# A planner's two rules in a kernel of attention and experts: when a side job may take its bank, and from when its result counts

## What is computed

```python
q, k, v = (split_heads(x @ W + b) for W, b in ((Wq, bq), (Wk, bk), (Wv, bv)))
attn = einsum(q, k) / sqrt(32) - slope[h] * (T - 1 - key)      # causal
x = layernorm(x + (softmax(attn) @ v) @ Wo + bo)
p = softmax(x @ Wr + br);  e = argmax(p)
y = (silu(x @ Wg[e]) * (x @ Wu[e])) @ Wd[e] * p[e]
x = layernorm(x + y)
```

## Time and profile before

| | us |
|---|---|
| median of 3 runs | 1257.86 (1256.21 to 1259.7) |
| the profiled execution, its own time | 1257.54 |
| its span, first to last instruction | 1255.8 |
| attention units | about 27 to 485 |
| tail between attention and experts | about 485 to 541 |
| experts | about 541 to 1240 |

### The profile page before, as it was taken

One profiled execution on the slowest core, in us unless ns is written; L12 is line 12 of the kernel. 1 busy time (PEld: TensorE's weight loads), 2 busy tenths in 40 slices (PEclk: granted clock), 3 DMA queues, 4 the chain that ended last, 5 costly groups with the idle time before them and its releaser, 6 DMA issues.

```text
span 1255.8 us, 27816 instructions
## 1 busy us (share of the span) xinstructions
PE 1165.1 (93%) x8697; PEld 1063.2 (85%) x8697; DVE 768.6 (61%) x1978; ACT 570.4 (45%) x1395; POOL 307.3 (24%) x443
## 2 busy tenths in 40 slices
PE   6998998999899987499999999999999999999994
PEld 5888888887888875498998899899989988998993
DVE  3676767676767776456546655664665465456665
ACT  4676766765666673043323332332333232323344
POOL 5400201201020122353213311330331133123336
PEclk9999999999999998589999999999999999999997
DMA  8223223222322240271322223122313222231302
GB/s 274 62 52 79 71 67 103 54 60 68 94 52 64 68 123 35 61 200 44 93 68 62 75 79 91 51 85 68 93 51 91 72 60 76 72 98 51 85 33 103
DMA packets 109685, 100.11 MB, mean 80 GB/s; under 512 B 12847, under 2 KB 81839, under 8 KB 109552
## 3 DMA queue, kind: packets, MB, share of 16 engines
q1 hardware_dynamic: 104784, 87.85, 24.8%
q0 software_dynamic: 3040, 9.18, 2.2%
q10 hardware_dynamic: 1728, 1.31, 0.3%
HBM read 64.74 MB, written 9.18 MB: 59 GB/s over the span
## 4 chain that ended last, share of the span: by engine, by line
PE 76%; DVE 6%; POOL 5%; ACT 4%; issue 4%; DMA 3%; SPq 1%; ACTq 0%; DVEq 0%; POOLq 0%
PE bank L805 35%; PE bank L583 14%; PE bank L830 10%; PE bank L721 4%; PE bank L704 4%; POOL up_lo L1455 4%; PE bank L817 3%; PE bank L693 2%; DMA up_raw<-in_Wu_dram 2%; SPq L475 1%; ACT probs L913 1%; DVE probs L1153 1%; PE bank L730 1%; PE bank L681 1%; ACT up_hi L945 1%
## 5 line engine op out<-in xcount | busy, mean ns | idle before, releaser
L805 PE MATMUL bank<-up_hi,xsT_hi 128*128 x1216 | 356.2, 293 | 5.7 <-POOL up_lo L1455 4.6
L805 PE MATMUL bank<-up_lo,xsT_hi 128*128 x1216 | 344.6, 283 | 0.0
L805 PE MATMUL bank<-up_hi,xsT_lo 128*128 x1216 | 344.5, 283 | 0.0
L1455 POOL TENSOR_TENSOR up_lo<-up_raw,up_hi 128x256 fp32r<-128x256 f32 x241 | 169.9, 741 | 477.8 <-ACT up_hi L945 477.6
L1294 DVE SCALAR_TENSOR_TENSOR h_tok<-bank,row_weight,silu 128x128 f32<-128x128 f32 x304 | 93.4, 347 | 292.3 <-ACT silu L1009 292.3
L805 PEld LDWEIGHTS bank<-up_hi,xsT_hi 128*128 128x128 f32 x1216 | 233.0, 192 | 12.3 <-issue 12.0
L805 PEld LDWEIGHTS bank<-up_hi,xsT_lo 128*128 128x128 f32 x1216 | 233.7, 192 | 0.3
L805 PEld LDWEIGHTS bank<-up_lo,xsT_hi 128*128 128x128 f32 x1216 | 233.1, 192 | 0.0
L1009 ACT ACTIVATE silu<-bank 128x256 f32<-128x256 f32 (+1 forms) x160 | 59.6, 373 | 364.5 <-PE bank L805 364.5
L1311 DVE TENSOR_TENSOR y<-bank,y 128x512 f32<-128x512 f32 x295 | 198.5, 688 | 0.5
L913 ACT ACTIVATE probs<-probs,neg_max 128x512 f32<-128x512 f32 (+3 forms) x256 | 136.5, 558 | 56.4 <-DVE neg_max L1153 55.4
(11 more groups left out here) (168 smaller groups left out, 2083.8 us busy)
## 6 DMA issues: line engine op xcount, KB each, us to landing
up_raw<-in_Wg_dram SPq DMA_DIRECT2D x64, 256.0 KB, 3.5
up_raw<-in_Wu_dram SPq DMA_DIRECT2D x64, 256.0 KB, 4.1
down_raw<-in_Wd_dram SPq DMA_DIRECT2D x64, 256.0 KB, 2.7
k_stack<-qk_hi SPq DMA_DIRECT2D x128, 64.0 KB, 2.0
q_stack<-qk_hi SPq DMA_DIRECT2D x128, 64.0 KB, 2.0
k_stack<-qk_lo SPq DMA_DIRECT2D x64, 64.0 KB, 2.0
q_stack<-qk_lo SPq DMA_DIRECT2D x64, 64.0 KB, 2.0
x_tok<-in_x_dram SPq DMA_DIRECT2D x3, 1024.0 KB, 5.5
```

Of the source, the lines that this page charges most:

```text
L805: mm = pe.matmul(bank[:, n * 2 * P:(n + 1) * 2 * P], a[:, s, k, :], up_w[w][k][:, :, :].rearrange("p a f -> p (a f)")[:, bass.ds(at, 2 * P ...
L1455: pool.tensor_tensor(up_w[1][k][:, e, :], up_raw[:, idx % NUPS, k, :, :].rearrange("p g f -> p (g f)"), up_w[0][k][:, e, :].bitcast(F32), ...
```

## The change

A bank that a job is to take must now have been flushed in an earlier unit for half 0, and in this unit or earlier for half 1 (`plan.flushed.get(prior, U) + (1 - half) > u` refuses it). And results flushed in unit u enter `ready` only after half 1 of unit u, so they can be used from unit u+1 on; in the last units (from 186) they still enter between the halves. Everything else, the jobs, their sizes and the budget, stays. No instruction is added or removed; the side jobs of units 36 to 179 move by half a unit to several units, and a few jobs change places in the row (`OP` 0 goes behind `V` 3,1; `logit` 0 and `logit` 3 go behind `Q` 7 and `V` 4,1). The next sequence has the same moves 48 units later.

```diff
--- before.py
+++ after.py
@@ -168,7 +168,9 @@
             if not left:
                 if any(k not in ready for k in needs(queue[0])):
                     return
-                if any(plan.bank[j] == len(plan.number) % 2 for j in pending):
+
+                prior = plan.used.get(len(plan.number) % 2)
+                if prior is not None and plan.flushed.get(prior, U) + (1 - half) > u:
                     return
                 now_job = queue.popleft()
                 plan.add(now_job, 2)
@@ -231,10 +233,13 @@
             work(u, 0, owed() / (PER_GROUP - step))
         if u > VLAG + PER_HEAD + 2 and (u - VLAG - 3) % PER_HEAD == 0:
             ready.add(("o", (u - VLAG - 3) // PER_HEAD - 1))
+
+        if u >= U - PER_GROUP // 2:
+            ready.update(fresh)
+        if u < U:
+            work(u, 1, owed() / (PER_GROUP - step))
         ready.update(fresh)
         fresh.clear()
-        if u < U:
-            work(u, 1, owed() / (PER_GROUP - step))
     plan.rest = list(left) and [(now_job, left[0][0])] or []
     plan.rest_jobs = list(queue)
     plan.pending = list(pending)
```

## The result

| | before | after |
|---|---|---|
| median | 1258.78 (4 runs, 1256.21 to 1266.14) | 1243.01 (4 runs, 1240.69 to 1246.4) |
| ratio of runs | | 0.9868, 95% interval 0.9844 to 0.9893 |
| profiled execution, span | 1255.8 | 1244.6 |
| waits of PE for DVE's side takes, units 37 to 179 | 20.9 in 23 | 6.6 in 11 |
| start of unit 37 to start of unit 180 | 350.4 | 335.5 |

The forecast was 1245.5, range 1238 to 1255. The change gains 15.8 us by the medians. The last two rows of the table come from the starts of PE's score rows in the timeline; they say that the whole gain, 14.9 us in this profile, lies in the units whose side work moved. The profiled execution of the changed kernel reached unit 37 3.4 us later than that of the kernel before (104.2 against 100.8), in code that the change leaves alone; so its span shows less than the stretch does.

What follows compares the result with a forecast made beforehand. PE, working in order, was taken to set the pace, its idle waits for DVE's takes being winnable. Terms 12.45 + 2.1 (clock) - 2.2 (new waits) = 12.35 off 1257.86 gave 1245.5 us, range 1238 to 1255.

Steps and rivals of the forecast that it cites:

- What bounds the kernel: Units from 100 to 452 us: PE sets the pace; its waits for DVE's side takes are 20.9 us, 24.4 with allowance.
- xT and K, first sequence: Units 37 and 38: the xT pair in half 1 saves 0.45 us, K one half later 0.4, together 0.85.
- OT to OP 3 and the router rows: Units 58 to 87, again 106 to 135: shorter waits from moved jobs, 0.7, 2.35, 0.3 and 1.7 us a sequence.
- DVE's backlog at xT: Units 84 to 87: DVE can no longer catch up in PE's long stops, so waits of 0.5, 1.1 and 0.7 us.
- New waits: Units without side work go from 15 to 23; eight more at 0.27 us waiting for ACT cost 2.2 us.
- Clock: Granted clock falls at 302.4 and 333 us both go with shorter stops: 2.1 us gained, ends 0 and 3.1.
- Last sequence: Units 152, 162, 164 and 176: 1.5 us less of the 3.3 us of waits there.
- x in time: x load issued one iteration later, at 80, stays hidden: some 7 us from issue to need, 1.5 us to spare.
- The signs: Expected if right: waits 8 to 12 us, `OP` 2 under 0.6, `logit` 2 0.7 to 1.1, stretch some 12 us shorter.
- The waits move and do not go: Rival, chance 0.17: DVE's row begins no sooner, so the next job waits what the last saved; 1252.5 us.
- All vanish: Rival, chance 0.05: DVE runs ahead as PE's row is spread out, 24.4 + 2.1 us goes; 1231 us.
- the slower side: Clock rival, chance 0.07: light PE stretches at bare units make the clock fall, up to 1.54 us each; 1264 us.

Runs made afterwards that it cites:

- the first rule alone: Kernel before with only the bank change: a bank may be taken one half later, results still count from the flush's own unit; ratio 0.9887.
- `xT` moved back: Changed kernel with the bank condition lifted for the four xT jobs, so the second pair stands in half 0 again; one run, 1243.59 us.
- moments late: Changed kernel with DVE's moments of an OP placed behind the biased scores, not ahead; ratios 0.9846 and 0.9854, medians 1241.2 and 1240.9 us.
- x in parts: Changed kernel with the third and fourth sequence's x loads cut into four, each issued once its quarter's last reading OP is taken; 1243.3 us.

## Why the prediction was right, and where its steps were off

The direction, the place and the mechanism were right: 1243.0 lies in the range, 2.5 under the forecast. By its own steps:

- **What bounds the kernel.** Right. 14.3 of the 20.9 us of waits went, and the stretch is 12.7 shorter besides the clock.
- **xT and K, first sequence: 0.85.** Measured 0.55. The 0.45 for the `xT` pair was wrong: with the first rule alone it is 0.01, and with `xT` moved back nothing is lost. All of it is the bare unit put into the 3.88 us in front of `K`.
- **OT to OP 3 and the router rows: 5.05 a sequence** (0.7 + 2.35 + 0.3 + 1.7), less 1.1 for new waits, 3.95. Measured 5.0 and 5.6 in units 49 to 97, and in 97 to 145 8.05, of which the kernel before lost 2.2 to the clock: 5.9. The stops before `OP` 1, `OP` 2 and `OP` 3 did not shrink to 0.15, 0.46 and 0.4, they vanished, and `logit` 2 kept 0.33 and not 0.8. (The single stretches of 12 units can't be set against the terms: `OP` 0 and `logit` 3 moved across their borders.)
- **DVE's backlog at xT**: 0.5, 1.1 and 0.7 were put at units 84, 85 and 86 to 87; the rows have 0, 0.47 + 0.82 and 0.76. Right in kind and size.
- **New waits: 2.2.** This term was mis-sized. It took one stop of 0.27 for each new bare unit; ACT's exponentials cost 0.2 in all, and the products with v 0.26 and 0.35 (units 169 and 178) outside the units already counted. Together with the stops at `OP` and `logit`, two points up, it makes up the 2.5 to 3.1 by which the stretch was better than 12.35.
- **Clock: 2.1.** Right: 1.55 and, from units 121 to 133 of the kernel before being 0.63 longer than 73 to 85, 0.6; and both profiles of the changed kernel have no fall there. Not every fall comes back at its place, so a profile of the kernel before may hold more or fewer.
- **Last sequence: 1.5.** Measured 1.25.
- **x in time.** Right in outcome, by 0.2 us; the working took the landing time of the kernel before, 5.5 us, and here it was 6.5.
- **The signs.** Four of its six signs of being right came: `OP` 2's stop under 0.6, the `xT` stops as long as before, the stretch shorter (14.9, put at some 12), the experts unchanged. Two did not, both on the side of too little gain: the waits for side takes sum to 6.6 and not 8 to 12, and `logit` 2 waits 0.33 and not 0.7 to 1.1. By the medians the gain is 15.8, 3.4 more than the 12.35 of the sum. That the number is only 2.5 off is in part luck: with its fourth run the median of the kernel before came out 0.9 higher.
- **The rivals.** "The waits move and do not go" holds for the `xT` chain and was seen nowhere else. "All vanish" did not come, and the slower side neither: 23 bare units, no fall.

## What to carry to other kernels

When an in-order engine stops for a result that another engine is just about to take, place the job by what the taking engine has in front of it, not by when the producer is done: here half a unit of other work, together with a take that no longer stood behind 0.9 us of DVE's own work, ended a whole stop of 1.8 us. Before moving a job, find out whether its stop is a lone wait or a link in a serial chain (start to start stayed at 3.87 to 3.88 us in three kernels): there only work put inside the chain counts. And follow what else is released by the moved step; one more half unit of delay made a load late and cost all it had won.

## What the runs showed of the hardware that was not expected

- The same stop of 1.76 us on PE was followed by a fall (3.6 us at a mean granted clock of 0.53 and 0.55) in one of two places in one profile, and in the other of the two in the next; each cost 1.54 to 1.55 us. The stop alone does not decide it.
- Between profiles unit starts repeat to 0.01 to 0.05 us over stretches of 30 us, while over the fourteen profiles the time from the start to unit 37 differed by up to 4.4 us (99.8 to 104.2) and the time from unit 180 to the end by up to 4.8 (802.7 to 807.5). Differences of 1 us between plans can be read from a single profile, if units 49 to 61 and falls of the clock are set aside, though not from four timed runs.
- Units 49 to 61 are the exception: -1.6 to -2.9 over the profiles in which the second rule holds. The traces point at a load: ACT's copy of `K` 5, at unit 50, waits until the last stack load of the group before has landed, and ACT, which works in order, has the softmax's copies behind it. In the changed kernel (unit 50 starts at 135.60), then with `xT` moved back (131.45):

```profile
138.43 0.69 ACT L893 ACTIVATE qk_hi<-bank,bias_col 128x512 fp32r<-128x512 f32 x1 [2.92 <-DMA q_stack<-qk_lo]
```

```profile
132.80 0.69 ACT L893 ACTIVATE qk_hi<-bank,bias_col 128x512 fp32r<-128x512 f32 x1 [1.44 <-DMA q_stack<-qk_lo]
```

  The copy starts 2.83 and 1.35 into unit 50, and units 49 to 61 take 25.31 and 24.40 us. The six profiles with this plan in these units (the changed kernel and its repeat, moments late twice, `xT` back, x in parts) stand in the same order by both: 1.35, 2.01, 2.05, 2.22, 2.83 and 3.05 into the unit; 24.40, 24.53, 24.55, 24.71, 25.31 and 25.53 us. In the two profiles of the kernel before the copy starts at the unit's start or 0.4 into it, and the units take 27.28 both times. So up to 1.1 us of the change's gain hangs on when this load lands, 2.0 to 3.9 us after its issue; what slows the load is open, and no run changed it alone.
